# First attention of a two-layer block: row maxima spread over all steps, values and sums of a pair of steps in one PSUM bank

## The reference, cut to what matters

```
A1 = einsum("bhqd,bhkd->bhqk", Q1, K1) * scaling   # dh = 16
A2 = einsum("bhqd,bhkd->bhqk", Q2, K2) * scaling
A1 = where(causal, A1, -inf); A2 = where(causal, A2, -inf)
attn = softmax(A1, -1) - lam * softmax(A2, -1)
O = einsum("bhqk,bhkd->bhqd", attn, V)              # V has 32 columns
```

## Time and profile before

| | us |
|---|---|
| Median of 3 runs | 4366.25 |
| Lowest, highest | 4363.6, 4369.36 |
| The profiled execution, its own time | 4362.48 |
| Its span, first to last instruction | 4360.6 |
| Mean granted clock of TensorE, full is 1 | 0.911 |

### The profile page before, as it was taken

How to read it: one execution, slowest core, us unless ns; L and a number is a source line. 1 busy time by engine, 2 the same in 40 slices (tenths; PEclk the granted TensorE clock), 3 DMA queues, 4 the chain that set the end, 5 groups by cost and what they waited for, 6 DMA issues and landing times. The chain is left out here.

```text
span 4360.6 us, 69689 instructions
## 1 busy us (share of the span) xinstructions
PE 3700.6 (85%) x21166; PEld 1647.8 (38%) x21231; DVE 2467.0 (57%) x4628; ACT 1754.4 (40%) x3522; POOL 1706.6 (39%) x1117
## 2 busy tenths in 40 slices
PE   6869999999999999999999996753899678896794
PEld 3322333232323232323233323642455445555462
DVE  4456766575757576767676753767211276666102
ACT  2324665666656566666666663110122141111110
POOL 1313555555555555555555554400344231110203
PEclk9978999999999999999999997855899899996897
DMA  4431111111111111111111103210443200001332
GB/s 156 154 120 33 34 37 33 34 35 35 35 35 35 35 35 35 35 36 34 38 33 38 31 9 96 82 40 0 121 91 76 45 24 4 0 0 39 111 111 87
DMA packets 202326, 224.92 MB, mean 52 GB/s; under 512 B 86673, under 2 KB 162706, under 8 KB 195858
## 3 DMA queue, kind: packets, MB, share of 16 engines
q1 hardware_dynamic: 186642, 195.39, 15.3%
q0 software_dynamic: 15360, 25.44, 3.1%
HBM read 139.12 MB, written 80.87 MB: 50 GB/s over the span
## 5 line engine op out<-in xcount | busy, mean ns | idle before, releaser
L638 POOL TENSOR_TENSOR attention_probs<-attention_probs 128x1024 f32<-128x1024 f32 (+2 forms) x640 | 1228.1, 1921 | 1160.2 <-PE attention_ps_o L791 1160.1
L708 DVE TENSOR_REDUCE attention_chunk_max<-attention_ps_m 128x1 f32<-128x512 f32 (+3 forms) x2560 | 1394.2, 604 | 457.4 <-PE attention_ps_m L823 280.6
L683 ACT ACTIVATE attention_probs<-attention_ps_s 128x512 f32<-128x512 f32 (+3 forms) x2560 | 1199.5, 532 | 826.9 <-PE attention_ps_s L772 459.7
L768 PE MATMUL attention_ps_s<-attention_q_stack,attention_k_stack 99*128 99x512 bf16 (+3 forms) x2560 | 821.6, 354 | 91.1 <-ACT attention_probs L683 70.1
L820 PE MATMUL attention_ps_m<-attention_k_stack,attention_q_stack 96*128 96x512 bf16 (+3 forms) x2560 | 772.5, 357 | 48.7 <-DMA attention_v_head<-v_rows 34.5
L791 PE MATMUL attention_ps_o<-attention_probs,attention_v_head 128*32 128x512 f32 (+3 forms) x5120 | 647.4, 558 | 8.6 <-issue 5.0
L768 PEld LDWEIGHTS attention_ps_s<-attention_q_stack,attention_k_stack 99*128 99x128 bf16 x2560 | 234.0, 98 | 668.4 <-ACT attention_probs L683 466.0
L820 PEld LDWEIGHTS attention_ps_m<-attention_k_stack,attention_q_stack 96*128 96x128 bf16 x2560 | 224.9, 97 | 628.7 <-DVE attention_chunk_max L708 490.2
L809 PE MATMUL attention_ps_l<-attention_probs,consts 128*32 128x512 f32 (+1 forms) x2560 | 352.6, 580 | 9.7 <-POOL attention_probs L638 1.0
L734 DVE TENSOR_TENSOR attention_out_sb<-attention_even_sb,attention_odd_sb 64x512 f32<-64x512 f32 x128 | 115.0, 898 | 296.8 <-ACT attention_even_sb L656 290.9
L823 PE MATMUL attention_ps_m<-mask_q_bf,ident_bf 128*128 128x128 bf16 x1024 | 225.5, 223 | 0.0
(11 more groups left out here) (283 smaller groups left out, 4108.8 us busy)
## 6 DMA issues: line engine op xcount, KB each, us to landing
qk_parts<-project_parts SPq DMA_DIRECT2D x64, 384.0 KB, 3.0
heads_out<-attention_out_sb SPq DMA_DIRECT2D x128, 128.0 KB, 2.3
out_heads<-heads_out SPq DMA_DIRECT2D x8, 2048.0 KB, 8.2
experts_w<-in_f_w SPq DMA_DIRECT2D x16, 1024.0 KB, 8.3
attention_q_stack<-qk_parts SPq DMA_DIRECT2D x32, 384.0 KB
attention_k_stack<-qk_parts SPq DMA_DIRECT2D x32, 384.0 KB
experts_w<-in_e_w SPq DMA_DIRECT2D x24, 512.0 KB, 4.8
v_rows<-project_v SPq DMA_DIRECT2D x8, 1024.0 KB, 4.2
```

Of the source, the lines that this page charges most:

```text
L638: pool.tensor_tensor(probs[:, to, :, lo:], probs[:, to, :, lo:], probs[:, k % RING_P, :, lo:], ALU.add).then_inc(pair_ok, 1)
L683: act.activation(probs[:, k % RING_P, a, left(k):], ps_s[(2 * k + a) % RING_S][:, left(k):], ACT.Exp, scale=float(DH) ** -0.5).then_inc(pr ...
L708: last = dve.tensor_reduce(chunk_max[:, a, jq, c:c + 1], ps_m[m % RING_M][:, 0:width(m)], AX.X, ALU.max)
L768: last = pe.matmul(psum[:, lo:], ks[at][0:WITH_MAX, a, kb * P:(kb + 1) * P], qs[at][0:WITH_MAX, a, tq * GROUP + lo:(tq + 1) * GROUP], star ...
```

## The change: what it does

Maxima: steps 0 to 17 now compute the rest of the next head's maxima, and steps 20 to 39 begin with those of the head after the next: 42 of the 80 in the last 20 steps, 38 in the first 18. The maxima are turned at step 18. In TensorE's order they stand in thirds after the first score of an iteration, after the second, and at its end.

Values and sums: the four strips are now two score sets by two halves of the queries (blocks of 128 queries, even and odd ones), so one step fills the four strips with 256 queries each, and one pair of steps does so for the sums. Values and sums of a turn lie in one bank, of which there are two. The products that cleared a bank, the two copies of values and VectorE's addition of halves are gone: ScalarE copies one bank, 128 x 512, in one go. It does so at step `LAST + 4`, between the step's two exponentials, and for that it waits for the store of two turns ago and for the last sums. SP stores a turn with four DMAs in place of two, and its order is now load, turn 3 of the head before, turns 0 and 1, parts, turn 2.

```diff
-QUAD = 4
+PAIR = 2
+BLOCKS = GROUP // P // 2
-FIRST_MAX, LAST_MAX, TURN_MAX = 2, 32, 32
+BEGIN_MAX, END_MAX = 20, 18
...
+        def maxima_at(head, k, after, later):
+            early, steps_early = len(MAXIMA) * (N_STEPS - BEGIN_MAX) // (N_STEPS - BEGIN_MAX + END_MAX), N_STEPS - BEGIN_MAX
+            if k >= BEGIN_MAX:
+                n = k - BEGIN_MAX
+                return later, range(n * early // steps_early, (n + 1) * early // steps_early)
+            start = 0 if is_first(head) else early
+            n, rest = min(k, END_MAX), len(MAXIMA) - start
+            return after, range(start + n * rest // END_MAX, start + min(k + 1, END_MAX) * rest // END_MAX)
...
-                for turn in range(Q_TILES):
+                for turn in range(Q_TILES - 1):
                     if head is not None and not (is_first(head.n) and turn == 0):
                         store(head.n, turn)
...
+                if head is not None:
+                    store(head.n, Q_TILES - 1)
...
+                wait_apart(sp, taken, head * Q_TILES + turn + RING_O, core.passed)
+                for half in range(2):
+                    rows = slice(half * 2 * DV, (half + 1) * 2 * DV)
+                    sp.dma_start(oT[ds(h, 1), :, tile * GROUP:(tile + 1) * GROUP].rearrange(
+                        "n e (u v t) -> v (n e) u t", v=2, t=P)[half], results[rows, slot, 0]).then_inc(stored[slot], 16)
+                    sp.dma_start(sums[ds(h, 1), :, tile * GROUP:(tile + 1) * GROUP].rearrange(
+                        "n e (u v t) -> v (n e) u t", v=2, t=P)[half],
+                        results[half * 2 * DV:(half + 1) * 2 * DV:DV, slot, 1]).then_inc(stored[slot], 16)
...
+                    act.wait_ge(stored[slot], (head * (Q_TILES // RING_O) + turn // RING_O + 1) * (STORES * 16))
+                act.wait_ge(values_ok, head * N_STEPS + LAST[turn] + 1)
+                act.wait_ge(ones_ok, head * PAIRS + (LAST[turn] + 1) // PAIR + RING_P // PAIR)
+                act.activation(results[:, slot], ps_o[slot][:], ACT.Copy).then_inc(taken, 1)
...
                     for a in range(2):
+                        ended = ends(k, 4)
+                        if a == 1 and ended and not (ended[1] and is_first(head)):
+                            take(head - 1 if ended[1] else head, ended[0])
...
+            def strips(k):
+                first = left(k) // P
+                for half in range(2):
+                    block = (first - half + 1) // 2
+                    if block < BLOCKS:
+                        for a in range(2):
+                            yield (half * 2 + a) * DV, half, a, block
...
+                for strip, half, a, block in strips(k):
+                    last = pe.matmul(psum[strip:strip + DV, 0, block:], vh[at][:, kb], halves(k, a, half, block),
+                                     start=kb == 0, stop=False, tile_position=(0, strip), skip_group_check=True)
...
                     values(head, at, k)
+                    values(head, at, k + 1)
+                    if k > 0:
+                        ones(head, k // PAIR - 1)
```

185 lines of the change are left out of this document (62 added, 123 removed).

## The result

The changed kernel takes 4486.98 us (median of four executions, 4478.79 to 4498.43), the kernel before 4367.01 us (4363.6 to 4369.36) beside it on the same chip: a ratio of 1.0277, 95% interval 1.0253 to 1.0302. It is slower, as forecast, and 54 us above the forecast of 4433: a loss of 120 us where 67 were forecast. That lies inside the stated range of 4310 to 4540, and 7 us above the forecast's own of 4390 to 4480.

What follows compares the result with a forecast made beforehand. TensorE was taken to bound the second part, the store's wait the first: 31.7 + 41.0 + 1.7 = 74.4 us a head against 72.25. 4362.5 + 62 - 12 + 17 = 4429.5, median 3.8 above: 4433; range 4310 to 4540, its own 4390 to 4480.

Steps and rivals of the forecast that it cites:

- The wait for the store: Copy of turn 1, at step 15, waits for a store queued behind the load; values 14 at +31.7 us, 29 heads.
- the head's first part: From the previous head's last values to values of step 14: 31.7 us against 31.1, some 7 idle for TensorE.
- The clock: After TensorE's idle stretch in mid-head, 1.2 GHz loses at least 1.7 us a head.
- second part: From values of step 14 to the head's end: 39.1 us, with joints and banks 41.0, against 40.7 before.
- The joints: Between TensorE's passes in strips: 0.027 us each, 100 a head in place of 30, plus 0.1 an iteration for new weights.
- The banks: Three banks for maxima, the fourth product waiting for VectorE's reduction: 0.06 us an iteration, at most 0.2.
- The heads that are not among the 29: First head about +7 us, head 30 without late maxima -8, heads 30 and 31 without the wait -7 and -4: together -12.
- dear joints: Rival: new weights cost near 0.41 us an iteration, or 1.2 GHz lasts twice as long; 4540 us, chance 0.2.
- The cheap one: Rival: the wait but no other cost, joints 0.027, banks never short; 72.5 us a head, 4379 us, chance 0.2.
- The one of a store in time: Rival: the store lands before +24 us, copy 15 does not wait; 66.5 us a head, 4186 us, chance 0.15.

Runs made afterwards that it cites:

- e1_slots: The changed kernel with four result buffers in SBUF in place of two: 4285.77 us, 0.9823 of the kernel before.
- e3_swap: The changed kernel with SyncE issuing the store of the previous head's fourth turn ahead of the load: 4345.85 us, 0.9973 of the kernel before.
- e8_wide: The changed kernel with each strip of queries and keys loaded by its own DMA, 13 loads in place of 7: 4273.62 us, 0.9797 of the kernel before.
- e11_b22: The changed kernel with the maxima of the head after next beginning at step 22, not 20: 4424.92 us, 1.0149 of the kernel before.
- e2_place: The changed kernel with an iteration's maxima placed as before: behind the second score, behind the strips' group, at the end: 4355.08 us, 0.9967 of the kernel before.
- e4_maxima_alone: The kernel before with only the even spread of the maxima and the change's SyncE order: 4427.68 us, 1.0145 of the kernel before.

## Why the prediction was right, and where its sum was off

**The wait for the store** was foreseen in place, count and size. 29 heads have it, as said; the store's issue ends 26.6 us after the load (said: 25 to 27), the copy starts 30.2 us after it (said: 29.8), and the head's first part, to the values of step 14, is 0.7 us longer than before (means of 32.5 against 31.8 us, taken in the same way; said: 0.6). e1_slots shows that without it the change is no loss, and e3_swap and e8_wide that it comes from a store queued behind a load on few engines.

**The clock** was put at 1.7 us a head, from the earlier trace rows. In steps 14 to 16 the changed kernel takes 5.11 us and e1_slots, whose clock stays full there in all 27 heads, 3.45: 1.66. At a head's end the clock falls in 4 of the 27 heads, where it was 24 before; in the middle it falls in all 27, as foretold.

**The step that failed: a term that the sum did not have.** It is the stand at steps 18 to 20: 4.68 us where before it was 2.73. The prediction's second part, 41.0 us and the clock, had maxima, scores and strips as TensorE's work with 0.06 us an iteration for short banks, and never asked what else VectorE has to do when the maxima of the head after next begin: its count of 48 us a head is under the period, but the four short instructions on the turned maxima now stand ahead of reductions for which TensorE waits. e11_b22 puts 56 to 62 us on it, against the 54 us by which the forecast was short. That the two are near each other is in part luck, since the other errors nearly cancel.

**Two terms were mis-sized, in opposite directions.** The joints, put at 0.027 each and 0.1 an iteration more, cost 0.027 an iteration in all (a strip's third pass stands 0.22 us behind its second, and not 0.24 as foretold): some 0.2 us an iteration too dear, 2.5 us over the second part. The banks, put at 0.06 an iteration with 0.2 as the most, cost 2.5 us over the nine iterations of steps 20 to 38 (e2_place), 0.28 each. The bank is taken for 1.17 us (1724.93 to 1726.10; said: 1.15). But TensorE is at the fourth maximum after 0.82 us and not after 0.93, since the average maximum that I put between holds the narrow ones too: a narrow maximum in the middle does not relieve the bank, it brings the fourth product sooner. The 0.2 was no upper bound.

**The heads that are not among the 29** were put at -12 us together. With the stretch before the first values they came to about +3, above all since the first head, with all 80 maxima in 18 steps, takes 87.6 us where it took 70.1: 17 us more, and not 7; why is not shown. So some 15 of the 54 us lie there, and some 40 in the 29 heads: the missing stand and the banks, less what the joints were put at too much.

**The rivals.** That of dear joints is refuted; nothing of the weight loads that it would show is seen here. The cheap one, 4379 us, had the wait, the clock and the joints right, and the banks wrong; these and the missing stand refute it. The one of a store in time, 4186 us, was wrong in its condition, and too low for its own case: e1_slots, which removes the wait, gives 4286. Removing the wait does bring a gain over the kernel before, but 81 us and not 180, for the same missing stand and the banks. With the places mended too it is 4126.

**Still open**: the price of the banks is read from moved products and their lateness; a kernel with four banks for maxima was not tried, as all eight are in use. The same lateness stands in steps 0 to 8 (0.24 to 0.38 us in four of the iterations), where the prediction had it covered by the wait for the store; its price there is not measured. The split of steps 18 to 20 between the stretched cast (0.66 us) and the chain's mere place is not measured either: in e11_b22 and e2_place the cast is stretched as before (0.93 and 0.92 us), and only what stood behind it has moved away.

## What to carry to other kernels

A buffer that is stored is free only when the queue has got to its store, so before a change makes the engines faster, look at what the queue holds ahead of it, and keep as many buffers as the longest issue needs (two more took 201 us off). Where work is moved to begin right behind a small serial chain on an engine, ask who waits for that engine's next result: two steps of distance were worth some 60 us here. And where products share three banks, look at how close a fourth stands, whatever the average load says: other places for the same products were worth 132 us.

## What the runs showed of the hardware that was not expected

- Passes in column strips follow each other without a gap once a group runs: of the joints in four passes of 256 columns (0.88 us) only the first 0.027 us can be read, though every strip gets new weights and all use the same rows. The Trainium skill (TensorE: Matmul & The Clock Gate, "Part 3: Packing small matmuls") says that a weight load overlaps running matmuls only where the row groups differ, by which each load would show; the measurement decides.
- A cast and a subtraction of 32 x 128 elements in SBUF on VectorE take 1.35 and 1.79 us in e4_maxima_alone, beside GpSimd's additions, and 0.25 and 0.28 us in the kernel before (all medians).
- A store's issue stands 21.28 us behind a load in 7 DMAs, during most of which the DMA share is near 0.2; behind the same bytes in 13 DMAs at a share near 1 it stands 6.59 us, and 0.65 us with no load ahead of it.
